# Two attention heads share one product with the plain counts; groups of five tiles instead of three and four

## The reference, cut to what matters

```python
ft = jnp.einsum('nhd,od->nho', hv, W)
a1 = jnp.sum(ft * attn_l, axis=-1)
a2 = jnp.sum(ft * attn_r, axis=-1)
e = jax.nn.leaky_relu(a1[src] + a2[dst], negative_slope=NEG_SLOPE)
w = jnp.exp(e - m[dst])
denom = jax.ops.segment_sum(w, dst, num_segments=n)
alpha = w / jnp.maximum(denom[dst], 1e-16)
agg = jax.ops.segment_sum(alpha[:, :, None] * ft[src], dst, num_segments=n)
out = jax.nn.relu((agg + res).reshape(n, H * DOUT))
```

## Time and profile before

| | us |
|---|---|
| median of 3 runs (lowest, highest) | 999.89 (999.59, 1002.16) |
| the profiled execution | 999.84 |
| its span, first to last instruction | 998.0 |

### The profile page before, as it was taken

One profiled execution on the slowest core, in us unless ns is written; L12 is line 12 of the kernel. 1 busy time (PEld: TensorE's weight loads), 2 busy tenths in 40 slices (PEclk: granted clock), 3 DMA queues, 4 the chain that ended last, 5 costly groups with the idle time before them and its releaser, 6 DMA issues.

```text
span 998.0 us, 15944 instructions
## 1 busy us (share of the span) xinstructions
PE 978.0 (98%) x5726; PEld 792.6 (79%) x5726; DVE 597.3 (60%) x1280; ACT 312.3 (31%) x890; POOL 67.5 (7%) x135
## 2 busy tenths in 40 slices
PE   8999999999999999999899999999999999999998
PEld 6777678999999999986566666666998557988895
DVE  8987899999999999996233238551111111432422
ACT  3444354655565566444101112221111111101101
POOL 2100000000000000123122210000000000000000
PEclk9999999999999999999999999999999999999999
DMA  6000010111111111008582439114001003411002
GB/s 164 2 1 1 1 57 18 36 39 39 43 45 46 48 45 38 14 22 293 167 324 96 152 148 302 56 51 147 1 1 47 1 1 89 113 32 31 16 16 64
DMA packets 40172, 70.00 MB, mean 70 GB/s; under 512 B 21103, under 2 KB 25205, under 8 KB 39602
## 3 DMA queue, kind: packets, MB, share of 16 engines
q1 hardware_dynamic: 37423, 58.81, 18.7%
q0 software_dynamic: 2080, 10.23, 3.0%
q10 hardware_dynamic: 611, 0.20, 0.1%
HBM read 50.10 MB, written 19.12 MB: 69 GB/s over the span
## 4 chain that ended last, share of the span: by engine, by line
PE 89%; DVE 7%; issue 1%; ACT 1%; DMA 1%; POOL 0%; DVEq 0%; SPq 0%; POOLq 0%
PE O L983 19%; PE pw L1161 16%; PE pw L1225 7%; PE pa L1190 7%; PE pc L851 7%; PE O L980 7%; PE ph L1076 5%; PE py L1100 5%; PE pw L1254 4%; PE pa L1237 4%; PE pf L816 2%; DVE ohs_a L1645 2%; PE pt L1149 1%; PE pf L851 1%; DVE ohd L1642 1%
## 5 line engine op out<-in xcount | busy, mean ns | idle before, releaser
L983 PE MATMUL O<-X,masks 125*125 125x260 f32 x1200 | 276.6, 329 | 0.0
L980 PE MATMUL O<-X,CSR 125*125 125x130 f32 x1080 | 244.6, 227 | 0.0
L983 PEld LDWEIGHTS O<-X,masks 125*125 125x125 f32 x1200 | 221.3, 187 | 0.1
L1838 DVE SCALAR_TENSOR_TENSOR masks<-a2b,NA,CSR 125x375 fp32r<-125x375 f32 (+1 forms) x360 | 211.6, 650 | 5.6 <-PE O L983 4.3
L980 PEld LDWEIGHTS O<-X,CSR 125*125 125x125 f32 x1080 | 203.6, 189 | 0.0
L2103 DVE SCALAR_TENSOR_TENSOR UL<-pw,dinv,UH 125x768 fp32r<-125x768 f32 x20 | 20.4, 1018 | 107.7 <-ACT UH L1564 107.7
L1161 PE MATMUL pw<-W 128*125 128x384 f32 x240 | 79.1, 486 | 0.8 <-ACT W L1557 0.8
L851 PE MATMUL pc<-ohs_a,ohd 125*125 125x512 f16 x375 | 77.4, 345 | 0.8 <-DVE ohs_a L1645 0.8
L1161 PE MATMUL pw<-region,xr_or_h 128*125 128x384 f32 x240 | 77.6, 486 | 0.0
L1161 PEld LDWEIGHTS pw<-region,xr_or_h 128*125 128x125 f32 x240 | 45.0, 188 | 32.1
L1645 DVE TENSOR_SCALAR ohs_a<-iota,srcf 125x1250 f16<-125x1250 f16 x128 | 69.6, 544 | 0.0
(11 more groups left out here) (259 smaller groups left out, 1434.4 us busy)
## 6 DMA issues: line engine op xcount, KB each, us to landing
a2b<-a_rows SPq DMA_DIRECT2D x12, 610.4 KB
W<-in_L_ffn_W SPq DMA_DIRECT2D x4, 1152.0 KB, 6.5
WM<-in_L_ffn_W SPq DMA_DIRECT2D x4, 1152.0 KB, 10.2
xr_or_h<-in_x SPq DMA_DIRECT2D x10, 336.0 KB
XH<-in_x SPq DMA_DIRECT2D x12, 280.0 KB
z_rows<-region SPq DMA_DIRECT2D x10, 336.0 KB
region<-y_rows SPq DMA_DIRECT2D x10, 336.0 KB
x_rows<-xr_or_h SPq DMA_DIRECT2D x10, 336.0 KB
```

The costliest lines, as they stand in the source:

```text
L980: nc.tensor.matmul(O[0:P, bank, d - d0, 2 * DP:4 * DP], CSR[:, s, d * P:(d + 1) * P], X[:, buf, s, 4:6, :].rearrange("p k d -> p (k d)"), ...
L983: ins = nc.tensor.matmul(O[0:P, bank, d - d0, 0:4 * DP], kept, X[:, buf, s, 0:4, :].rearrange("p k d -> p (k d)"), start=s == 0, stop=s == ...
L1838: nc.vector.scalar_tensor_tensor(masks[:, s, 0:(d1 - d0) * P], a2b[:, buf, d0 * P:d1 * P], NA1[:, s, bass.ds(h, 1)], CSR[:, s, d0 * P:d1 * ...
```

## The change

- Heads 1 to 10 form five pairs. In the first head of a pair (PAIR, the odd one) the plain product takes the second products of both heads, X[:, 0:2, s, 4:6, :], 260 columns; the first two quarters of the bank receive the next head's part. The masked product goes to the last four quarters. In the second head (PAIRED) there is no plain product: ScalarE has copied the next head's part out of the banks into `ahead` (one copy more at each eviction of PAIR), and PE starts each bank of PAIRED with a product of `ident` with `ahead` (float32, 130 columns).
- Heads 1 to 10 go in two groups of five target tiles (FIVES). Their ten tiles lie in eight banks: the tiles of SHARED, 0 and 1 of the first group and 8 and 9 of the second, use the same banks 3 and 4. PE does them first in the last s of a group, which s_half tells ScalarE, and last in the first s of the next.
- Masks are 625 columns wide, 20 a head, in 8 slots instead of 10.
- The products and high and low parts are counted for first and second product apart, since PAIR needs the second product of the next head at its own start: `low_part(1, h + 1)` stands behind the fourth mask of PAIR, and PE waits for it before it begins PAIR.
- `combine` works in place in `sums`; its five steps stand behind masks 0, 1, 2, 7 and 9 of the second group. The new `low_part(0)` stands behind mask 4 there, and `low_part(1)` in PAIRED behind mask 5.
- There is one buffer of x columns, asked for one head later; the last head's goes into `ahead`.
- Heads 0 and 11 keep the old groups.

PE and ScalarE (cut):

```diff
+                    def head(h, buf, kind):
+                        def plain(s, d, bank):
+                            nc.tensor.matmul(bank[:, 0:4 * DP], CSR[:, s, d * P:(d + 1) * P],
+                                             X[:, 0:2, s, 4:6, :].rearrange("p b k d -> p b (k d)"),
+                                             start=False, stop=False, skip_group_check=True)
+                        pe.wait_ge(s_lo[0], h + 1)
+                        pe.wait_ge(s_xn, h + 1)
+                        if kind == PAIR:
+                            pe.wait_ge(s_lo[1], h + 2)
+                        for g, (d0, d1) in enumerate(FIVES):
+                            own = [d for d in range(d0, d1) if d not in SHARED[g]]
+                            pe.wait_ge(s_ev, 4 * h + (-1, 1)[g])
...
+                                        for d in own:
+                                            nc.tensor.matmul(bank_of(d)[:, 2 * DP:4 * DP], ident[0:P, 0:P], ahead[:, d, :],
+                                                             start=True, stop=False, skip_group_check=True)
...
+                    def pair(q, last=False):
+                        h = 2 * q + 1
+                        products(act, 0, h + 1)
+                        products_high(act, 0, h + 1, 0)
+                        negated(act, h + 1, 0)
+                        evict_five(h, 1, 0, q)
+                        products(act, 0, h + 2)
+                        scale_rows(h - 1, 0)
+                        evict_five(h, 1, 1, q)
+                        products(act, 1, h + 2)
+                        products_high(act, 1, h + 2, 1)
+                        products_high(act, 0, h + 2, 1)
+                        evict_five(h + 1, 0, 0)
+                        negated(act, h + 2, 1)
                         if not last:
-                            products(act, h + 1, 1 - buf)
-                        if not first:
-                            scale_rows(h - 1)
-                        evict(h, buf, 0)
-                        evict(h, buf, 1)
-                        if not last:
-                            negated(act, h + 1, 1 - buf)
+                            products(act, 1, h + 3)
+                            products_high(act, 1, h + 3, 0)
+                        scale_rows(h, 1)
+                        evict_five(h + 1, 0, 1)
```

VectorE (cut); `negated(act, h)` waits for `low_part(1, h)`, `products(act, n, h)` for `low_part(n, h - 1)`:

```diff
+                    def head(h, buf, kind):
+                        row_in(h, buf)
+                        for s in range(NT):
+                            mask(h, buf, 0, s, FIVES)
+                            if kind == PAIR and s == 3:
+                                low_part(dve, 1, h + 1, 0)
+                        steps = combine(h - 1, 1 - buf, False)
+                        for s in range(NT):
+                            mask(h, buf, 1, s, FIVES)
+                            if s in (0, 1, 2, 7, 9):
+                                next(steps)
+                            if s == 4:
+                                low_part(dve, 0, h + 1, 1 - buf)
+                            if kind == PAIRED and s == 5:
+                                low_part(dve, 1, h + 1, 1 - buf)
```

`evict_five` does the two shared tiles first, after s_half (two copies, since their banks lie in different halves, two more into `ahead` in PAIR, two scalings), then the three others (one copy, one more in PAIR, three scalings). SyncE:

```diff
                     for h in range(2, H):
                         row(h, h % 2)
-                        x_columns(h)
-                    sp.wait_ge(s_ev, JOBS * H + 2)
+                        sp.wait_ge(s_xa, h)
+                        x_columns(h - 1, XH, s_xh)
+                    sp.wait_ge(s_ap, 2 * (H // 2))
+                    x_columns(H - 1, XH_last, s_xi)
+                    sp.wait_ge(s_ev, 4 * H)
```

More of the change, by code:

```diff
@@ L213, in products_high @@
[L213 to L218, removed]
-        def negated(act, h, buf):
[L221 to L230, removed]
+        s_xn = sem("products_negated")
@@ new lines, in program, with products, product_of @@
+        s_t, s_hi, s_lo = ([sem(f"{w}_{n}") for n in ("first", "second")]
+                           for w in ("products", "products_high", "products_low"))
+        def products(act, n, h):
+            if not (isinstance(h, int) and h == 0):
+                act.wait_ge(s_lo[n], h)
+            for s in range(NT):
+                product_of(n, h, s)
+        def product_of(n, h, s):
+            nc.scalar.mul(T12[:, n, s, :], FT[:, s, h, :], (E1, E2)[n][:, s, bass.ds(h, 1)]).then_inc(s_t[n], 1)
@@ new lines, in alone @@
+                                order = list(range(d0, d1))
+                                if h and not g and not s:
+                                    order = order[1:] + order[:1]
+                                for d in order:
+                                    bank = O[0:P, half, d - d0, :]
+                                    if h and not g and not s and d == d0:
+                                        pe.wait_ge(s_ev, 4 * h)
+                                    if s:
+                                        plain(s, d, bank)
+                                    ins = masked(h, buf, g, s, d, d0, bank, s == 0)
@@ L998, in quickly @@
+                    alone(0, 0)
+                    pe.wait_ge(s_ev, 4)
+                    with pe.Fori(0, H // 2 - 2) as q:
+                        head(2 * q + 1, 1, PAIR)
+                        head(2 * q + 2, 0, PAIRED)
+                    head(H - 3, 1, PAIR)
+                    head(H - 2, 0, PAIRED)
+                    alone(H - 1, 1)
+                    pe.wait_ge(s_ev, 4 * H - 1)
                     turn_z(0)
@@ L1495, in quickly @@
+                    with act.Fori(0, H // 2 - 2) as q:
+                        pair(q)
+                    pair(H // 2 - 2, last=True)
+                    evict(H - 1, 1, 0)
+                    scale_rows(H - 2, 0)
+                    evict(H - 1, 1, 1)
                     copy_zt(0)
@@ L1716, in _ @@
                     if n == 185:
-                        low_parts(dve, 0, 0)
+                        for u in range(2):
+                            low_part(dve, u, 0, 0)
                     if n == 190:
@@ L1905, in quickly @@
                     dve.wait_ge(s_ctf, 3 * (NT - 1))
-                    head(0, 0, first=True)
-                    with dve.Fori(0, H // 2 - 1) as q:
+                    dve.sem_inc(s_xa, 1)
+                    alone(0, 0)
+                    with dve.Fori(0, H // 2 - 2) as q:
                         k.loop(q, 6)
-                        head(2 * q + 1, 1)
-                        head(2 * q + 2, 0)
-                        k.end(H // 2 - 1)
-                    head(H - 1, 1, last=True)
+                        head(2 * q + 1, 1, PAIR)
+                        head(2 * q + 2, 0, PAIRED)
+                        k.end(H // 2 - 2)
```

286 lines of the change are left out of this document (181 added, 105 removed).

## The result

The changed kernel takes 1039.48 us (median of 4 runs, 1038.31 to 1041.83), the kernel before 1000.87 beside it; the ratio is 1.0389 with a 95% interval of 1.0364 to 1.0413. It is slower by 38.6 us; 1038 was forecast. The profiled execution took 1038.31 us, its span is 1036.4.

The account below looks back on a forecast made before the run. The prediction took a loop of waits through PE, ScalarE and VectorE to bound the heads, 52.9 us a pair. Added to 999.9 us, +30 before the clock and +8 for its falls gave 1038 us, range 1006 to 1056.

Parts of the forecast that it names:

- The loop: Heads 1 to 10: waits through PE, ScalarE and VectorE make a pair 52.9 us, 6.9 more than before.
- Its two waits: VectorE's fourth combine step waits for ScalarE's scale_rows once in PAIR and once in PAIRED, 5.4 and 5.3 us.
- The four pieces of the pair: To PAIR's scaling 19.4 us, to VectorE's last low part 19.6, to PAIRED's scaling 6.9, to next PAIR 7.0.
- The copies: ScalarE's one-tile copies at PAIR's evictions, a shape the trace lacks: about 0.2 us each, bounds 0.1 and 0.38.
- PE's work: PE needs 37.7 us a pair, 8.3 less than before; rival that this work bounds: 958 us, chance 0.06.
- The clock: PE's idle stretches drop its clock to 1.2 GHz at PAIR's start: four times 2 us, +8.
- The row of early products: Earlier trace's start: 12 products took 3.98 us, later 2.30; basis for about 1.7 us a clock fall.
- last pair: Fifth pair, without the products in PAIRED and with head 11 following: 45.9 us, so -0.1.
- The sum: Whole stage of heads: +30 us before the clock, +38 with it; rival without falls 1030 us, chance 0.18.
- start of head 1: After head 0 PE waits for a high part and a low part: +1.9 us.
- head 11: The last head begins behind VectorE: +0.7 us.
- What was charged at nothing: Evictions in front of PE (about 0.9 us), SyncE's transfers, heads 0 and 11, all later stages: no added time.

Follow-up runs that it names:

- e1_scale_first: Changed kernel with scale_rows(h) in PAIRED moved on ScalarE ahead of negated(h + 2), products(1, h + 3) and their high part; 1020.19 us.
- e2_scale_early_pair: Changed kernel with scale_rows(h - 1) in PAIR moved on ScalarE ahead of products(0, h + 2), behind the first group's eviction; 1034.31 us.
- e3_both_orders: Changed kernel with scale_rows moved ahead of the products on ScalarE in both PAIR and PAIRED; 1010.83 us.
- e4_low_part_early: Changed kernel with scale_rows moved earlier in PAIR and PAIRED, and low_part(1, h + 1) behind PAIR's first mask instead of its fourth; 999.15 us.
- e9_masks_narrow: Changed kernel with masks of 375 instead of 625 columns in heads 1 to 10, two fifths of the masking left out; 1020.12 us.
- e12_narrow_filled: Kernel of e10_early_filled with masks of 375 columns in heads 1 to 10, two fifths of the masking left out; 981.57 us.
- e6_idle_filled: Changed kernel with PE's idle stretches in PAIRED filled by products that nobody reads; 1037.12 us.
- e10_early_filled: Kernel of e4_low_part_early with unread products in PE's idle stretches: 7 after head 0, 5 ending each PAIRED, 10 behind head 11; 992.36 us.

## Why the prediction was right

**The loop.** Forecast for a pair before the clock: 52.9 us. Measured where the clock is up at the start of PAIR: 53.25 (the first pair of the changed kernel) and 53.28 (filled). Its two waits were put at 5.3 and 5.4 us; nine of the ten are 5.46 to 5.94, and the last one, where three us of products are left out ahead of the scaling, is 2.2. The four pieces of the pair shown above, which begins at 243.78: the scaling of PAIR ends 20.7 us later, at 264.45 (19.4 forecast, and the clock's 1.4); the low part ends 19.7 us after that (19.6), the scaling of PAIRED ends 6.9 after the low part (6.9), and the next PAIR starts 7.4 after the scaling (7.0).

```profile
261.93 2.52 ACT L1592 ACTIVATE sums<-sums,rec 125x64 f32<-125x64 f32 x10
```

The experiments test the same loop. In the table the pair is as measured, behind it the time from its start for which the granted clock is still at the lower level, and then the pair less half of that time, which is what half the rate loses in it (pairs that are followed by another):

| kernel | forecast, clock up | pair (at 1.2 GHz) | less half |
|---|---|---|---|
| changed | 52.9 | 54.65 (3.2) | 53.1 |
| `e1_scale_first` | 47.5 | 50.10 (5.5), 49.12 (3.1) | 47.4, 47.6 |
| `e2_scale_early_pair` | 51.0 | 52.82 (2.9), 53.60 (4.7), 54.01 (5.8) | 51.3, 51.2, 51.1 |
| `e3_both_orders` | 45.5 | 47.95 (4.6), 45.92 (0) | 45.7, 45.9 |
| `e4_low_part_early` | 43.2 | 44.93 (2.9), 43.58 (0) | 43.5, 43.6 |
| `e9_masks_narrow` | 47.5 | 50.63 (6.1), 49.35 (3.3), 47.89 (0) | 47.6, 47.7, 47.9 |
| `e12_narrow_filled` | 41.7 | 41.85 (0) | 41.9 |

Each lies within half a microsecond of its forecast.

Single steps: VectorE's mask of 625 columns was put at 872 ns, as an extension of the earlier trace rows, and is 864; the stretch of ScalarE from `negated` to the end of the scaling at 6.9 us, and is 6.85 (284.21 to 291.06).

**The copies.** The one shape that no row showed, a copy of one tile, was taken at 0.2 us between 0.1 and 0.38. The trace after has steps of 0.16:

```profile
256.87 0.27 ACT L1580 COPY sums<-O 125x130 f32<-125x130 f32 x1 [10.21 <-PE O L985]
257.03 0.28 ACT L1582 COPY ahead<-O 125x130 f32<-125x130 f32 x1
```

Four of them are on the loop, 0.2 us less than told.

**PE's work.** Taken: 0.122 us for 260 columns, and 0.111 for an identity product. The first is right (0.12, from 302.20 to 302.33). The second is half of what it should be. A float32 product leaves two records in the trace; the three identity products of the own tiles are the line with x6, the two of the shared tiles the one with x4, and the 50 of the whole kernel are 100 records:

```profile
269.72 0.83 PE L1051 MATMUL O<-ahead,ident 125*125 125x130 f32 x6
270.62 0.71 PE L1055 MATMUL O<-ahead,ident 125*125 125x130 f32 x4
L1051 PE MATMUL O<-ahead,ident x60: 272/273/276, 215.1 to 441.8; 125*125 125x130 f32 x60
```

A record has a step of (0.83 - 0.27) / 5 = 0.11 us, so a product takes 0.22: the value that the prediction named and didn't take. The earlier trace rows were read the same way: their 0.222 us is the step of a record, and the 60 products of L816 leave 120. PE's work is 38.8 us a pair and not 37.7, 7.2 less than before and not 8.3. It was of no matter to the time: this work was not what the pair waited for, which the doubled identity products and the filled idle time both show.

**The clock.** Forecast: four falls of 2 us, +8. Measured: five, +6.7 in all, about 1.36 us each. The row of early products gave the right order, and the fifth fall, behind the last pair, was missed: there the idle stretch is only 2.9 us long, behind ten products. The changed kernel was lucky at its start too. PE is idle for the same 1.9 us between head 0 and the first PAIR in eight of the traces; the clock fell there in three (`e1_scale_first`, `e2_scale_early_pair`, `e4_low_part_early`) and not in the changed kernel.

**The sum.** Told and found, in us: start of head 1 +1.9 and +2.1; first pair +6.9 and +7.2; three pairs 3 x 6.9 and the clock's 2 each, 26.7 in all, and 3 x 8.6 = 25.8; last pair -0.1 and the fourth fall's 2, and +2.0; head 11 +0.7, and +1.4 with its fall. Together +38 and +38.4. The mechanism was right, and the closeness of the sum is in part luck: without the clock +30 was told and 38.4 - 6.7 = 31.7 found, and the clock was put 1.3 too high.

**What was charged at nothing.** The evictions in front of PE are there (0.8 us at PAIRED's first shared tile in the second group), and inside the stretch in which PE follows VectorE, as told: ScalarE's first copy could be late, since PE waits for masks anyway. SyncE's transfers never show as a wait. The stages behind the heads kept their 556.2 us, but not for the reason told: PE starts them 1.5 us late behind VectorE, is still 1.0 late at its last product, and the stretch from there to the end happens to be 1.0 shorter (next table).

**What was told wrong.** PE's work, as above. PE's idle time in the stage was put at over 60 us; by the windows it is 315.65 - 263.25 = 52.4. Of the difference 5.5 us are the identity products' second records; the rest wasn't taken apart (products at the lower clock, and the ends of products before each short gap, both count as busy).

**Behind the stage.** The forecasts of the experiments let all stages behind keep their length, and that is the term that failed in them. PE does the same 2393 products there in every kernel. When they start, in us from the end of the stage:

| kernel | first | 241st | last | end of the span |
|---|---|---|---|---|
| before | 0.0 | 37.6 | 551.4 | 556.2 |
| changed | 1.5 | 39.1 | 552.4 | 556.2 |
| `e2_scale_early_pair` | 2.3 | 39.9 | 553.1 | 558.3 |
| `e6_idle_filled` | 2.8 | 42.7 | 556.3 | 561.9 |
| `e4_low_part_early` | 2.8 | 42.3 | 557.1 | 560.9 |
| `e10_early_filled` | 2.8 | 40.4 | 555.3 | 560.0 |
| `e12_narrow_filled` | 2.8 | 40.4 | 553.6 | 558.4 |

Three things are in it. The first is PE's wait for VectorE, which hasn't normalised the first rows when head 11 ends: up to 2.8 us where PE ends it early, with ten products in the gap or without, and 0 before. The second is the clock: behind that wait it is at the lower level in `e4_low_part_early` and `e6_idle_filled`, and they lose 1.9 and 2.2 us by the 241st product, which `e10_early_filled` doesn't (the first line is of `e4_low_part_early`, the others are of `e10_early_filled`):

```profile
437.91 1.49 PE L926 MATMUL O<-ident,region 125*128 125x125 f32 x6 [2.81 <-DVE region L1878]
...
430.64 2.49 PE L963 MATMUL O<-CSR 125*125 125x512 f32 x10
433.62 0.83 PE L926 MATMUL O<-ident,region 125*128 125x125 f32 x6 [0.49 <-DVE region L1883]
```

A second fall, 44 to 49 us behind the stage, costs both `e4_low_part_early` and `e10_early_filled` 1.7 us more, and `e12_narrow_filled`, in which the clock stays up, nothing. The third is the stretch from the last product to the end, 3.8 to 5.6 us with the same instructions; what sets it wasn't looked for. So in `e10_early_filled` the wait is the greater part of the 3.8 us lost there against before, and the ten products in it don't shorten it.

## What to carry to other kernels

When two engines are near their limit, count the second one first: here PE could have given 7.2 us a pair (8.3 by the forecast), and VectorE only 3.8. Then follow the order of the third, idle one: ScalarE was busy half of the time and still set the pace, because a result that VectorE waits for stood behind work that waits for VectorE. Moving one call of `scale_rows` ahead of that work was worth 19 us, as much as leaving out two fifths of the masking. Filling PE's idle stretches paid where the clock fell in them, and only for what the fall had cost: in the changed kernel 6.7 us in the stage, of which the total shows 2.4, within its noise. And look at who has to be ready when a stage ends sooner: here PE then waited up to 2.8 us at the start of the next one.

## What the runs showed of the hardware

- The same product of 260 columns has a step of 0.22 us at 1.2 GHz and 0.12 at 2.4 GHz.
- A float32 product leaves two records, and takes 0.22 us for 130 columns; a masked or plain product (float32r) of twice as many columns takes 0.12.
- The clock fell in stretches of PE that I had held to be too short. In `e4_low_part_early` the idle stretches at the end of a pair are three, of 0.65, 0.66 and 1.58 us, with ten products between them, and it fell there in two pairs of four. With five products of 512 columns more in the last of them (`e10_early_filled`) it didn't fall in any. And one idle stretch of 1.9 us, the same in eight traces, was followed by a fall in three of them.
- A product that nobody reads can pay: 7 + 4 x 5 + 10 of them took 6.8 us off, from 999.15 to 992.36 (5.2 between the traced executions).
- GpSimd's subtract of 650 float32 elements a partition took from 1.7 to 6.8 us beside VectorE's masks, and each of the ten stretched exactly one mask, from 0.86 to about 2.08 us, while the masks before kept their step.
